# Counting edges in groups of 10 targets with three chunks each, two groups to a part

## What is computed

```python
edge_index = jnp.stack([src, dst])
xn = _layernorm(x, axis=-1)
x = x + _L0_gnn_ref(xn, edge_index, W, b) + _L0_mix_ref(xn[None], Wq, bq, Wk, bk, Wv, bv, Wo, bo)[0]
x = x + _L0_ffn_ref(_layernorm(x, axis=-1)[None], ...)[0]
# _L0_gnn_ref: h = x @ W; msg = h[src] * norm[:, None]
#              relu(segment_sum(msg, dst, num_segments=n) + b), loops added
# _L0_mix_ref: linear attention, phi = elu + 1; S = phi(K)^T V; Z = sum of phi(K)
```

## Time and profile before

| | us |
|---|---|
| three runs | 995.83, 996.22 (median), 997.37 |
| the profiled execution, its own time | 995.84 |
| its span, first to last instruction | 994.1 |
| TensorE busy | 975.2 (98%) |
| VectorE, ScalarE, GpSimd busy | 543.9, 293.6, 142.4 |
| matmuls of the counting (L1471), 400 | 108.7 to 283.4 |
| comparisons of the counting (L1076, L1077), 100 each | 418 and 421 ns each |
| evictions of the counting (L747), 100 | 283 ns each |

### The profile page before, as it was taken

How to read it: one execution, slowest core, us unless ns; L and a number is a source line. 1 busy time by engine, 2 the same in 40 slices (tenths; PEclk the granted TensorE clock), 3 DMA queues, 4 the chain that set the end, 5 groups by cost and what they waited for, 6 DMA issues and landing times.

```text
span 994.1 us, 13325 instructions
## 1 busy us (share of the span) xinstructions
PE 975.2 (98%) x4860; PEld 824.4 (83%) x4860; DVE 543.9 (55%) x1067; ACT 293.6 (30%) x585; POOL 142.4 (14%) x191
## 2 busy tenths in 40 slices
PE   5999999999999999999999999999999999999998
PEld 4887888888889989978786788767788999999986
DVE  6886578777763888782113556447557212122354
ACT  6873122232133343341213221114113312135300
POOL 7101001001011050050300000000201103064100
PEclk9999999999999999999999999999999999999999
DMA  7412013113021022122201465535422302010053
GB/s 269 150 49 86 5 30 117 28 31 100 16 77 36 26 90 73 52 69 95 96 12 55 147 204 172 157 119 186 170 80 90 123 1 85 1 43 1 22 190 139
DMA packets 46979, 86.78 MB, mean 87 GB/s; under 512 B 19036, under 2 KB 23388, under 8 KB 46896
## 3 DMA queue, kind: packets, MB, share of 16 engines
q1 hardware_dynamic: 38416, 57.28, 17.5%
q0 software_dynamic: 8480, 28.45, 8.7%
HBM read 61.62 MB, written 24.09 MB: 86 GB/s over the span
## 4 chain that ended last, share of the span: by engine, by line
PE 92%; DVE 3%; DMA 2%; ACT 1%; issue 1%; POOL 1%; SPq 0%; DVEq 0%; ACTq 0%; POOLq 0%
PE PS L1431 11%; PE PS L1433 11%; PE PS L1432 11%; PE PS L1552 9%; PE PS L1553 9%; PE PS L1554 9%; PE PS L1610 5%; PE PS L1612 4%; PE PS L1630 3%; PE PS L1631 3%; PE PS L1629 3%; PE PS L1471 2%; PE PS L1446 2%; PE PS L1683 2%; PE PS L1682 2%; PE PS L1681 2%
## 5 line engine op out<-in xcount | busy, mean ns | idle before, releaser
L1431 PE MATMUL PS<-ring,act_t 128*128 128x512 f32 (+1 forms) x480 | 194.7, 406 | 1.3 <-POOL ring L443 0.6
L1433 PE MATMUL PS<-ring,act_t 128*128 128x512 f32 (+1 forms) x480 | 190.7, 397 | 0.0
L1432 PE MATMUL PS<-ring,act_t 128*128 128x512 f32 (+1 forms) x480 | 190.3, 396 | 0.0
L1552 PE MATMUL PS<-act_t,ring 128*128 128x416 f32 (+1 forms) x432 | 159.3, 369 | 1.4 <-POOL ring L443 1.3
L1553 PE MATMUL PS<-act_t,ring 128*128 128x416 f32 (+1 forms) x432 | 152.2, 352 | 0.0
L1554 PE MATMUL PS<-act_t,ring 128*128 128x416 f32 (+1 forms) x432 | 151.7, 351 | 0.0
L1431 PEld LDWEIGHTS PS<-ring,act_t 128*128 128x128 f32 (+1 forms) x480 | 89.8, 187 | 23.9 <-POOL ring L443 1.6
L1433 PEld LDWEIGHTS PS<-ring,act_t 128*128 128x128 f32 (+1 forms) x480 | 89.5, 186 | 22.4
L1432 PEld LDWEIGHTS PS<-ring,act_t 128*128 128x128 f32 (+1 forms) x480 | 89.9, 187 | 21.2 <-issue 0.5
L1552 PEld LDWEIGHTS PS<-act_t,ring 128*128 128x128 f32 x432 | 81.3, 188 | 6.8 <-issue 3.4
L1553 PEld LDWEIGHTS PS<-act_t,ring 128*128 128x128 f32 x432 | 81.4, 188 | 4.0 <-issue 3.4
(11 more groups left out here) (195 smaller groups left out, 1650.7 us busy)
## 6 DMA issues: line engine op xcount, KB each, us to landing
stage_x<-in_wslices_dram POOLq DMA_DIRECT2D x54, 256.0 KB, 4.2
stage<-in_wslices_dram POOLq DMA_DIRECT2D x42, 256.0 KB, 3.7
xr<-x_d SPq DMA_DIRECT2D x18, 512.0 KB, 3.6
phin_d<-phiq SPq DMA_DIRECT2D x8, 625.0 KB, 3.1
xrow<-in_x_dram SPq DMA_DIRECT2D x9, 512.0 KB, 3.6
xh<-in_x_dram SPq DMA_DIRECT2D x18, 256.0 KB
x_d<-xh SPq DMA_DIRECT2D x18, 256.0 KB
x_d<-xr SPq DMA_DIRECT2D x9, 512.0 KB, 3.0
```

The source lines that it names most:

```text
L1431: pe.matmul(out_ap, node_rows(0, k, t), ring[:, slot(k0 + k), 0, :], start=(k == 0), stop=False)
L1432: pe.matmul(out_ap, node_rows(1, k, t), ring[:, slot(k0 + k), 0, :], start=False, stop=False)
L1433: ins = pe.matmul(out_ap, node_rows(0, k, t), ring[:, slot(k0 + k), 1, :], start=False, stop=(k == KD - 1))
L1552: pe.matmul(out_ap, w[0], x_t[:, 0, k, o:o + n], start=(k == 0), stop=False)
```

## The change

Groups get 10 targets and 3 x 128 edges in place of 13 and 4 x 128. A tile of 128 targets then has 13 groups, the last with 8 targets, and the last tile, with 98 rows, has 10: 127 groups. Two neighbouring groups make a part: VectorE compares for both with one instruction each for source (768 elements) and target (600), as three pairs of chunks; TensorE runs six matmuls of 100 columns into one bank; ScalarE evicts both together. A full tile is 7 parts (six of two groups, one of one), the last tile 5: 68 parts. Three parts go into a step, from step 12 to 34: two of them ahead of kv_sum, one behind. The one-hot slots go from 5 to 4, now larger. SyncE loads the keys of 13 groups a tile, each 3 x 128 edges. GpSimd has one memset less to do, VectorE one more (`kcur`, cleared once, since the last part of a tile reads a chunk past the keys).

```diff
-STATIC_CHUNKS = 4
+STATIC_CHUNKS = 3
-OH_BUFS = 5
+OH_BUFS = 4
-WIN = 13
+WIN = 10
-NWIN = NT * WPT
+NWIN = (NT - 1) * WPT - (-(N - (NT - 1) * P) // WIN)
+KEY_SLOTS = STATIC_CHUNKS * WPT + 1
...
+def groups_of(t):
+    return -(-rows(t) // WIN)
+PARTS = [(t, j, min(2, groups_of(t) - j)) for t in range(NT) for j in range(0, groups_of(t), 2)]
 def windows_of(step):
-    if 12 <= step < 37:
-        return list(range(4 * (step - 12), 4 * (step - 11)))
+    if 12 <= step < 35:
+        return list(range(3 * (step - 12), min(3 * (step - 11), len(PARTS))))
     return []
...
# SyncE, keys_load
-                for j in range(WPT):
+                for j in range(groups_of(dt)):
...
# ScalarE, adj_out
-                dt, j = divmod(w, WPT)
+                dt, j, m = PARTS[w]
...
# VectorE, constants and windows
+                link(dve.memset(kcur[:].rearrange("p a b c -> p (a b c)").bitcast(F32), 0.0))
...
-                dt, j = divmod(w, WPT)
+                dt, j, m = PARTS[w]
+                a = m + 1
...
-                dve.tensor_tensor(oh_src[:, b], count(P), pairs(kcur[:, dt % 2, j, 0], P), ALU.is_equal)
-                dve.tensor_tensor(oh_dst[:, b], count(WCOLS), pairs(kcur[:, dt % 2, j, 1], WCOLS),
-                                  ALU.is_equal).then_inc(onehot, 1)
+                dve.tensor_tensor(oh_src[:, b, 0:a], count(P), pairs(0, P), ALU.is_equal)
+                dve.tensor_tensor(oh_dst[:, b, 0:a], count(WCOLS), pairs(1, WCOLS), ALU.is_equal).then_inc(onehot, 1)
...
# TensorE, window
-                for j in range(STATIC_CHUNKS):
-                    n = width(w) * NT
-                    ins = pe.matmul(PS[:, b, 0:n], oh_src[:, o, j // 2, :, j % 2], oh_dst[:, o, j // 2, 0:n, j % 2],
-                                    start=(j == 0), stop=(j == STATIC_CHUNKS - 1))
+                _, j, m = PARTS[w]
+                for q in range(STATIC_CHUNKS * m):
+                    i, c = divmod(q, STATIC_CHUNKS)
+                    n = width(j + i) * NT
+                    ins = pe.matmul(PS[:, b, WCOLS * i:WCOLS * i + n], oh_src[:, o, q // 2, :, q % 2],
+                                    oh_dst[:, o, q // 2, 0:n, q % 2], start=(c == 0), stop=(c == STATIC_CHUNKS - 1))
```

More of the change, by code:

```diff
@@ L47 @@
 EX_COL = 64
-PAIRS = STATIC_CHUNKS // 2
-OH_BUFS = 5
+OH_BUFS = 4
 KEY_BUFS = 4
-WIN = 13
+WIN = 10
 WCOLS = WIN * NT
 WPT = -(-P // WIN)
-NWIN = NT * WPT
+NWIN = (NT - 1) * WPT - (-(N - (NT - 1) * P) // WIN)
+KEY_SLOTS = STATIC_CHUNKS * WPT + 1
 ROW_COLS = ROWL + 2
-THR_COL, FIRST_COL, FLAG_COL = 332, 340, 448
+THR_COL, FIRST_COL, FLAG_COL = 332, 340, 480
 CHUNKS = [(0, 418), (418, 416), (834, 416)]
@@ L151, in sums_of, with width, parts_through @@
     return step + 1 + (step + 1) // NT
-def width(w):
-    return min(WIN, P - w % WPT * WIN)
+def width(j, m=1):
+    return min(WIN * m, P - j * WIN)
+def parts_through(t):
+    return sum(p[0] <= t for p in PARTS)
 def tile_ended(step):
-    return [w // WPT for w in windows_of(step) if w % WPT == WPT - 1]
+    return [PARTS[w][0] for w in windows_of(step) if w + 1 == parts_through(PARTS[w][0])]
 def build(nc, x, src_rows, dst_rows, wslices, wo, bkv, bq, gb, bo, scales, w3s, out):
@@ L198, in build @@
         with ExitStack() as r2:
-            oh_src = sb("oh_src", [P, OH_BUFS, PAIRS, P, 2], BF16, r2)
-            oh_dst = sb("oh_dst", [P, OH_BUFS, PAIRS, WCOLS, 2], BF16, r2)
-            iota_2 = sb("iota_2", [P, WCOLS, 2], I16, r2)
+            oh_src = sb("oh_src", [P, OH_BUFS, STATIC_CHUNKS, P, 2], BF16, r2)
+            oh_dst = sb("oh_dst", [P, OH_BUFS, STATIC_CHUNKS, WCOLS, 2], BF16, r2)
+            iota_2 = sb("iota_2", [P, P, 2], I16, r2)
             kraw = sb("kraw", [P, KEY_BUFS, WPT, STATIC_CHUNKS, 2], F32, r2)
@@ L207, in build @@
             keys = sb("keys", [P, ROWL + EXTRA_CHUNKS, 2], F32, r2)
-            kcur = sb("kcur", [P, 2, WPT, 2, STATIC_CHUNKS], I16, r2)
+            kcur = sb("kcur", [P, 2, 2, KEY_SLOTS], I16, r2)
             cadd = sb("cadd", [P, 8, P], U16, r2)
@@ L215, in build @@
             ksum = sb("ksum", [P, D], F32, r2)
-            iota_c = sb("iota_c", [P, WCOLS], F16, r2)
+            iota_c = sb("iota_c", [P, P], F16, r2)
             ident_u = sb("ident_u", [P, P], U16, r2)
@@ L235, in build @@
             row_of = sb("row_of", [P, NWIN + 1], F32, r3)
-            thr = sb("thr", [P, NWIN + 1], F32, r3)
+            thr = sb("thr", [P, NT * WPT], F32, r3)
             thr_g = sb("thr_g", [P, 1], F32, r3)
@@ L242, in build @@
             sizes = sb("sizes", [P, NWIN + 2], F32, r3)
-            iota_i = sb("iota_i", [P, WCOLS], I32, r3)
+            iota_i = sb("iota_i", [P, P], I32, r3)
             kvb = sb("kvb", [P, 2, 512], F32, r3)
@@ L652, in _ @@
             nc.gpsimd.memset(st_blk[:], 0.0).then_inc(consts, 1)
-            nc.gpsimd.iota(iota_i[:], [[1, WCOLS]], base=0, channel_multiplier=0).then_inc(consts, 1)
-            nc.gpsimd.iota(thr[:, 0:NWIN].rearrange("p (a b) -> p a b", a=NT), [[P, NT], [WIN, WPT]], base=0, channel_multiplier=0,
+            nc.gpsimd.iota(iota_i[:], [[1, P]], base=0, channel_multiplier=0).then_inc(consts, 1)
+            nc.gpsimd.iota(thr[:].rearrange("p (a b) -> p a b", a=NT), [[P, NT], [WIN, WPT]], base=0, channel_multiplier=0,
                            allow_small_or_imprecise_dtypes=True).then_inc(consts, 1)
@@ L658, in _ @@
                            allow_small_or_imprecise_dtypes=True).then_inc(consts, 1)
-            nc.gpsimd.memset(thr[:, NWIN:], float(NT * P)).then_inc(consts, 1)
             for n in range(KD):
@@ L745, in adj_out @@
                     act.wait_ge(csum_ready, dt - 1)
-                n = width(w)
+                n = width(j, m)
                 nc.scalar.activation(
@@ L999, in edge_keys @@
                 dve.wait_ge(edges_in, 32)
-                dve.wait_ge(consts, 7)
+                dve.wait_ge(consts, 6)
                 link(dve.tensor_scalar(e_hi[:], e_src[:], 7, None, ALU.logical_shift_right))
@@ L1022, in edge_rows @@
                 link(dve.memset(first_d[0:1], -1.0))
-                link(dve.tensor_scalar(row_of[:], thr[:], first_d[:], None, ALU.is_gt))
-                dve.scalar_tensor_tensor(row_of[:], thr[:], d_row[:, ROWL:ROWL + 1], row_of[:], ALU.is_le,
+                link(dve.tensor_scalar(row_of[:], thr[:, 0:NWIN + 1], first_d[:], None, ALU.is_gt))
+                dve.scalar_tensor_tensor(row_of[:], thr[:, 0:NWIN + 1], d_row[:, ROWL:ROWL + 1], row_of[:], ALU.is_le,
                                          ALU.mult).then_inc(rows_known, 1)
@@ L1055, in group_keys @@
             def group_keys(dt):
-                dve.wait_ge(keys_got[dt], 16 * WPT)
-                dve.tensor_tensor(kcur[:, dt % 2], kraw[:, dt % KEY_BUFS].rearrange("p w c k -> p w k c"),
-                                  key_off[:, WPT * dt:WPT * (dt + 1), :].unsqueeze(3).to_broadcast([P, WPT, 2, STATIC_CHUNKS]),
+                g = groups_of(dt)
+                dve.wait_ge(keys_got[dt], 16 * g)
+                dve.tensor_tensor(kcur[:, dt % 2, :, 0:STATIC_CHUNKS * g].rearrange("p k (w c) -> p w k c", c=STATIC_CHUNKS),
+                                  kraw[:, dt % KEY_BUFS, 0:g].rearrange("p w c k -> p w k c"),
+                                  key_off[:, WPT * dt:WPT * dt + g, :].unsqueeze(3).to_broadcast([P, g, 2, STATIC_CHUNKS]),
                                   ALU.add).then_inc(kcur_ready, 1)
@@ L1070, in pairs @@
                 def pairs(k, n):
-                    return k.rearrange("p (a b) -> p a b", b=2).unsqueeze(2).to_broadcast([P, PAIRS, n, 2])
+                    at = kcur[:, dt % 2, k, STATIC_CHUNKS * j:STATIC_CHUNKS * j + 2 * a]
+                    return at.rearrange("p (a b) -> p a b", b=2).unsqueeze(2).to_broadcast([P, a, n, 2])
                 def count(n):
-                    return iota_2[:, 0:n, :].unsqueeze(1).to_broadcast([P, PAIRS, n, 2])
-                dve.tensor_tensor(oh_src[:, b], count(P), pairs(kcur[:, dt % 2, j, 0], P), ALU.is_equal)
-                dve.tensor_tensor(oh_dst[:, b], count(WCOLS), pairs(kcur[:, dt % 2, j, 1], WCOLS),
-                                  ALU.is_equal).then_inc(onehot, 1)
+                    return iota_2[:, 0:n, :].unsqueeze(1).to_broadcast([P, a, n, 2])
+                dve.tensor_tensor(oh_src[:, b, 0:a], count(P), pairs(0, P), ALU.is_equal)
+                dve.tensor_tensor(oh_dst[:, b, 0:a], count(WCOLS), pairs(1, WCOLS), ALU.is_equal).then_inc(onehot, 1)
             def all_counts(dt, more):
                 with dve.If(more > 0):
-                    for j in range(WPT):
-                        w = WPT * dt + j
-                        n = width(w)
+                    for j in range(groups_of(dt)):
+                        n = width(j)
                         to = ctile[:, dt % 2, :, j * WIN:j * WIN + n]
@@ L1092, in all_counts @@
                                 dve.tensor_scalar(ex_src[:, k, :], iota_c[:, 0:P], keys[:, at, 0], None, ALU.is_equal)
```

(18 more changed lines are left out.)

## The result

The changed kernel takes 1003.26 us (median of six runs, 1002.74 to 1003.64) against 996.72 us before (six runs, 995.36 to 997.59): ratio 1.0067, 95% interval 1.0054 to 1.0080. It is slower by 6.5 us; forecast was +5.4, 1001.6, in a range of 998.0 to 1004.5. The profiled execution took 1003.05 us, span 1001.2.

What follows compares the result with a forecast made beforehand. TensorE, busy 98% of the span, was taken to bound the kernel. Losses 2.2 (keys) + 6.7 (store) + 2.3 (clock) - 5.8 (counting gain) = +5.4 us on 996.22, forecasting 1001.6 us, range 998.0 to 1004.5.

Steps and rivals of the forecast that it cites:

- What bounds the kernel: TensorE, busy 98% of the span: time taken off its stream comes off the end, waits are added.
- Counting: TensorE's count matmuls in steps 12 to 34: fewer and narrower, 26.3 us down to 20.5, a gain of 5.8 us.
- A floor at 110 columns: TensorE's short matmuls: if spacing falls no lower than that of 110 columns, the gain is only 4.0 us.
- the pair cost: TensorE's count matmuls: if some 81 ns per load-and-matmul pair set the spacing, the gain is only 1.5 us.
- VectorE and ScalarE: Comparisons and evictions in the counting: 0.85 us a part against 1.35 for two windows, fewer evictions; costs nothing.
- The keys, first loss: Step 12: 13 key loads a tile, not 10, make keys late and TensorE resume at 111.15: loss 2.2 us.
- The store, second loss: Step 18: tile 0's store, behind 52 loads, lands at 152.6; ScalarE's eviction and TensorE wait: loss 6.7 us.
- The clock, third loss: After the 6.7 us stall TensorE resumes at 153.2 at half clock for 5 us: loss 2.3 us.
- rival (c): Key/value stage: SyncE becomes the bound, or spacing doesn't fall below that of 110 columns: 1003.1 to 1005 us, chance 0.15.
- (a): Counting gain without effect of SyncE's delay on ScalarE, with the late keys' loss: 992.6 us, chance 0.05.
- (b): The TensorE stalls come but the clock stays up: 999.3 us, chance 0.14.
- the tie at tile 1's store: SyncE's store of tile 1 lands at 167.5, ScalarE wants it at about 167.6: put at 0, up to 1.5 us.

Runs made afterwards that it cites:

- both edits: Changed kernel with parts in steps 13 to 35 and three tiles of key loads ahead of the first store: 991.34 us, 989.89 us when repeated.
- 46 and 49 loads: Changed kernel with the last 6, then the last 3, of its 52 first key loads put behind tile 0's store: 1002.55 and 1001.15 us.
- store sooner: Changed kernel with key loads of three tiles, not four, ahead of tile 0's store, later tiles' loads one store later: 992.84 us.
- the control: Kernel before with 30 key loads instead of 40 ahead of the first store, later tiles' loads one store later: 996.35 us, ratio 0.9999.
- the spare loads: Kernel before with 12 more key loads, into a tile nobody reads, behind its 40 first ones: 1008.35 us, ratio 1.0118.
- one step later: Changed kernel with all parts in steps 13 to 35: 1001.18 us, ratio 1.0047.

## Why the prediction was right

**What bounds the kernel:** right. The waiting in the stage stood in the span, 7.36 us at step 38 and 7.2 at the end; nothing later gave any back.

**Counting:** gain 5.8 forecast, 5.5 to 5.7 measured (5.4 in the changed kernel and 5.46 with both edits, and the 0.1 and 0.28 us by which their profiles were behind at 100 us). The spacing of 0.0465 us at 100 columns was 0.047. A floor at 110 columns (gain 4.0) is excluded by that row, and by the interval of the last ratio, which ends at 0.9952, where that gain would give 0.996. So is the pair cost of the Trainium skill (TensorE: Matmul & The Clock Gate, section "Back-to-back issue gap"), 81 ns for a load and a matmul of 128 columns: the trace disagrees, with 61 ns at 130 columns and 47 ns at 100.

**VectorE and ScalarE:** right, they cost nothing. A part takes VectorE 0.86 us (108.58 to 109.44; 0.85 forecast), an eviction of 200 columns 0.337 us. With both edits TensorE has no gap in the stage.

**The keys, first loss:** kcur at 108.25 (108.3), TensorE at 111.22 (111.15), idle 1.83 us (loss of 2.2 forecast). Missing was a term: the half clock behind it, 1.6 us. It came in five of the six profiles that have these gaps (the changed kernel twice, 46 and 49 loads, and one of the two of "store sooner"). I had tied the fall of the clock to one long gap; here it came behind two short ones, though not every time.

**The store, second loss:** 7.33 us against 6.7. The store was issued 0.8 us later than I had it (the loads began 0.4 us later than before, not 0.2; 52 of them took 1.11 us each, not 1.10; and from the issue of the biases to it were 0.8 us, not 0.5). It landed after 3.4 us, where the forecast took the median of all ten, 2.2, although this very store had taken 4.1 in the kernel before. So TensorE went on at 155.2, 2.0 us later than forecast. That the wait is only 0.6 us longer than forecast is luck: TensorE also got there later, at 147.9 instead of 146.5, held up by the half clock that I had missed. The wait lies inside the bounds given (6.0 to 8.6).

**The clock, third loss:** 2.0 us against 2.3 (4.4 us of it, 5 taken).

**The sum:** 1.83 + 1.6 + 7.33 + 2.0 - 5.46 = 7.3 at step 38, and +7.2 for the profiled execution (1003.05 - 995.84). That is 1.8 us above the forecast's 5.4. Item by item it looks like the first loss's clock (+1.6), but that isn't the cause. The first 52 loads and the store run on SyncE without waiting for TensorE (VectorE began to finish tile 0 at 131.6, 19.6 us before the store), and TensorE can't go on before the store has landed. Whatever holds TensorE up before that only shortens its wait: without the first loss and its half clock, the wait would by this working have been 3.4 us longer and the time the same (not run by itself). What made the kernel slower than forecast is the store, 2.0 us later, against 0.3 us less of half clock behind it. By the same reasoning the first loss costs something only once the store is in time, as in "store sooner" against both edits.

The measured 1003.26 us also lies in the band that was priced for rival (c), 1003.1 to 1005, though neither of its causes occurred. Of the rivals, (a) is refuted by the control, by the spare loads and by the wait itself; (b) by the clock's rows; (c) isn't what happened, but the run with 46 loads shows it is one step away: the tie at tile 1's store is real.

## What to carry to other kernels

A queue that only issues small transfers has a price an item; multiply it by the new count, and look what else stands in that queue, and who waits for it at second hand. Here a store that came 9 us late without harm had 3.7 us left, and 12 items of 1.1 us used them up. The slack must be read from the transfer in question: the median of ten gave 5.6. When a wait is removed, the next item of the same queue may be just behind it: move the whole sequence, not one piece. And a stall of several us can cost more than itself: here TensorE came back at half clock from each wait of over 4 us.

## What the runs showed of the hardware

- A key load through a register costs SyncE 1.10 to 1.11 us (44.06 us for 40, 57.54 for 52), though its transfer is 3 or 4 KB and lands in 1.6 us (median of both). Of that the issue is 0.33 us and the read of the start from `bounds` 0.27; register instructions and the pauses between them take the rest. 4 KB a load or 3 made no difference.
- The clock fell behind gaps far shorter than the 3.1 us at the end of the kernel before: after 0.63 and 1.20 us, one block of six short matmuls apart, in the changed kernel, after one gap of 1.8 us at 20 us in two profiles of twelve, and, outside the counting, after 0.57 + 0.76 us in three of twelve (one step later, the old counting with more loads, "store sooner" the second time). All twelve profiles have the gap at 20 us (1.6 to 1.8 us) and the pair, which lies at 359 to 378 us. It isn't the same each time for the same gaps; what decides was not settled here. Such a fall cost 3.4 x 0.465 = 1.6 us, more than the 1.2 us gap itself.
- Behind each of the six waits of 4.1 to 9.1 us (the changed kernel twice, one step later, the old counting with more loads, 46 and 49 loads) TensorE resumed at the lower level, and 4.0 to 5.4 us of its work ran there: 1.8 to 2.5 us lost. The clock had come down 2.1 to 5.0 us after TensorE stopped.
- The stores of the counts landed in 2.2 to 4.7 us in the changed kernel, and the one that mattered in 3.4; the same store took 4.1 in the kernel before, where the median was 2.2: a median is a poor guide for a single transfer.
